# Eight counted ranges in place of seven, 432 counted edge tiles in place of 404, and a larger VectorE budget per slot

## What is computed

```
dst = minimum((12500 * uniform((200000,)) ** 2).astype(int32), ...)   # then sorted
neigh = segment_sum(layernorm(x)[src], dst)            # sum over the edges
h = relu(((1 + eps) * layernorm(x) + neigh) @ W1 + b1) @ W2 + b2
x = x + batchnorm(h)                                   # needs all nodes
x = x + expert_ffn(layernorm(x))                       # routed to one of 8 experts
```

## Time and profile before

| | us |
|---|---|
| median of 3 runs | 2414.71 |
| lowest, highest | 2399.37, 2422.60 |
| the profiled execution | 2417.85 |
| its span, first to last instruction | 2416.2 |
| first gather starts | 118.0 |
| last gather starts | 1594.1 |
| edge stage ends, routing starts | 1629.5 |

### The profile page before, as it was taken

One profiled execution on the slowest core, in us unless ns is written; L12 is line 12 of the kernel. 1 busy time (PEld: TensorE's weight loads), 2 busy tenths in 40 slices (PEclk: granted clock), 3 DMA queues, 4 the chain that ended last, 5 costly groups with the idle time before them and its releaser, 6 DMA issues. The chain is left out here.

```text
span 2416.2 us, 34850 instructions
## 1 busy us (share of the span) xinstructions
PE 1752.9 (73%) x9215; PEld 1075.6 (45%) x9216; DVE 1395.7 (58%) x4228; ACT 917.1 (38%) x1445; POOL 1631.9 (68%) x1606
## 2 busy tenths in 40 slices
PE   0044566767776777778776887688968889799986
PEld 0022233333343333344433443348866556566664
DVE  7886642762753725525435332336865677857886
ACT  5931121431421413324223111116856455365643
POOL 1077777777777777777776777733655677568765
PEclk9998788878888888899898999995759989999998
DMA  6744458458457476584663663517932230321130
GB/s 222 264 136 121 139 166 277 140 164 278 140 183 259 131 246 219 175 267 120 194 212 111 207 197 106 149 47 224 283 126 90 91 93 19 101 90 57 63 100 23
DMA packets 186052, 376.43 MB, mean 156 GB/s; under 512 B 42806, under 2 KB 106636, under 8 KB 185831
## 3 DMA queue, kind: packets, MB, share of 16 engines
q1 hardware_dynamic: 118518, 198.24, 25.1%
q0 software_dynamic: 65168, 174.38, 23.7%
q10 hardware_dynamic: 2144, 1.05, 0.2%
HBM read 306.11 MB, written 71.64 MB: 156 GB/s over the span
## 5 line engine op out<-in xcount | busy, mean ns | idle before, releaser
L907 POOL DMA_INDIRECT space<-table,space x1159 | 1114.2, 961 | 392.4 <-issue 343.8
L1002 PE MATMUL e_sums<-space 128*128 128x256 f16 x1728 | 291.4, 341 | 301.9 <-DVE space L1279 143.6
L1002 PEld LDWEIGHTS e_sums<-space 128*128 128x128 f16 x1728 | 205.1, 121 | 395.4 <-issue 229.6
L1921 POOL TENSOR_TENSOR space<-space 128x512 f16<-128x512 f32 x200 | 293.9, 1495 | 109.0 <-ACT space L2055 103.7
L1268 DVE SCALAR_TENSOR_TENSOR space<-e_sums,above,space 128x256 f32 (+1 forms) x151 | 72.5, 480 | 487.5 <-PE e_sums L1002 329.2
L1163 ACT ACTIVATE counts<-e_tally 128x392 f32 (+1 forms) x296 | 203.9, 689 | 319.3 <-PE e_tally L1042 263.0
L1051 PE MATMUL e_tally<-w1f,counts 128*128 128x512 f16 x686 | 202.0, 424 | 130.7 <-DMA w1f<-table 130.3
L1331 DVE TENSOR_TENSOR counts<-counts,e_tally 128x98 f32 x296 | 175.0, 591 | 150.5 <-ACT counts L1163 105.7
L2011 PE MATMUL x_down<-space 128*128 128x256 f16 x2208 | 251.1, 276 | 14.9 <-DVE space L2148 13.0
L2055 ACT ACTIVATE space<-x_up,b_two 128x512 f32<-128x512 f32 (+1 forms) x400 | 249.0, 691 | 23.7 <-PE x_up L1987 13.9
L1987 PE MATMUL x_up<-space 128*128 128x512 f16 (+1 forms) x1200 | 252.1, 369 | 3.2 <-ACT space L2055 3.2
(11 more groups left out here) (214 smaller groups left out, 2334.9 us busy)
## 6 DMA issues: line engine op xcount, KB each, us to landing
w1f<-table SPq DMA_DIRECT2D x168, 512.0 KB
counts<-in_x SPq DMA_DIRECT2D x48, 512.0 KB, 4.9
space<-table,space POOLq DMA_INDIRECT x1159
slot_rows<-space SPq DMA_DIRECT2D x64, 268.0 KB
space<-slot_rows SPq DMA_DIRECT2D x32, 536.0 KB, 7.0
table<-space SPq DMA_DIRECT2D x25, 512.0 KB, 3.0
out<-space SPq DMA_DIRECT2D x24, 512.0 KB, 3.9
w1f<-in_w SPq DMA_DIRECT2D x8, 1024.0 KB, 5.1
```

What stands on the lines that cost most here:

```text
L907: pool.indirect_dma_start(got[:, r, t, :], None, table.rearrange("p h d -> (p h) d"), bass.IndirectOffsetOnAxis(ap=idx[:, h, first + t:fir ...
L1002: ins = nc.tensor.matmul(sums[:, place, 0:D], hot[:, place, t, :], got[:, r, t, half * D:(half + 1) * D], start=(t == 0 and half == 0), st ...
L1921: nc.gpsimd.tensor_tensor(midl[:, j % 2, c, :], midf[:, c % MB, :], midh[:, j % 2, c, :], ALU.subtract).then_inc(s_mlo, 1)
```

## The change

The counted tiles go from 404 to 432 in eight ranges, the due slots of the quads are earlier by 2 to 4, and the planner's budget for DVE goes from 9.6 to 11.2 us. No instruction is written anew.

```diff
-UNITS = (152, 64, 50, 41, 36, 32, 29)
+UNITS = (152, 64, 50, 41, 36, 32, 30, 27)
...
-CLOSE = {2: 19, 3: 30, 4: 39, 5: 48, 6: 55, 7: 63, 8: 69, 9: 76, 10: 82, 11: 88, 12: 94, 13: 99, 14: 104, 15: 109,
-         16: 114, 17: 118, 18: 123, 19: 127, 20: 132, 21: 136, 22: 140, 23: 144}
-TENSOR_ROOM, VECTOR_ROOM, BEHIND = 1040, 960, 300
+CLOSE = {2: 15, 3: 26, 4: 35, 5: 44, 6: 52, 7: 59, 8: 66, 9: 72, 10: 79, 11: 84, 12: 90, 13: 95, 14: 100, 15: 105,
+         16: 110, 17: 115, 18: 119, 19: 124, 20: 128, 21: 132, 22: 137, 23: 141}
+TENSOR_ROOM, VECTOR_ROOM, BEHIND = 1040, 1120, 300
```

## The result

| | before | changed |
|---|---|---|
| median, us | 2416.81 (4 runs) | 2450.84 (4 runs) |
| lowest, highest | 2399.37, 2422.60 | 2442.16, 2463.23 |
| profiled execution | 2417.85 | 2452.32 |
| first pieces begin | slot 20, 336.4 | slot 16, 297.0 |
| edge stage ends | 1629.5 | 1655.7 |

The ratio is 1.0157, interval [1.0113, 1.0201]: slower by 1.6%. The forecast was 2468, its range 2434 to 2505.

The account below looks back on a forecast made before the run. POOL's gathers looked like the bound, but PE and DVE's equally long chain would set the time: 296 + 1190 + 195 ends the edge stage at 1681, +51.5; 2417.85 + 51.5 = 2469, stated as 2468 us, range 2434 to 2505.

Parts of the forecast that it names:

- Two chains: Edge stage: POOL's gathers, 35 us less if unheld, and PE with DVE, which hold POOL about 100 us and set the time.
- Start of the chain: First 16 slots, 9 to 10 tiles each: POOL still paces them; pieces start in slot 16 at 296 us, not 336.4.
- Pieces: Stretches where table pieces are loaded and multiplied: eight in place of seven, 82 us each, 656 in all.
- second rival: Piece stretches: held POOL frees DMA engines, 77 us each, total 2429, within 1%; sign is stretches under 78; chance 0.13.
- Tiles of ranges 1 to 6: Counted-tile stretches: nearly the same tiles in 39 slots in place of 51, 461 us in place of 505.6.
- The slot: Tile stretches of ranges 1 to 6: each slot less saves its gathered group, 2.8 us (1.92 to 3.59); 12 save 34.
- The quarter: Tile stretches: each quarter less, four PE matmuls beside DVE's tiles, saves 0.6 us (0 to 1.2), 10 us in all.
- Range 7: The added eighth range's tile stretch: 27 wide tiles in 5 slots, 73 us, priced from range 6's 84.5.
- Sum of the chain: Slots 16 to 123: 656 + 461 + 73 = 1190 us for 107 slots, 11.1 each, where POOL needs 1070.
- Rest of the stage: Last 19 slots of the edge stage: 195 us in place of 200.7, so the stage ends at 1681, +51.5.
- Rival 3: Slots with 7 or 8 tiles: one more 3.00 us counting stall each, half showing, 42 us, total 2510; chance 0.12.
- Rival 4: Plan refused on the device, general path runs, if a range spans over 128 targets; 0.02 left out.

Follow-up runs that it names:

- second profile: The changed kernel run again unaltered, beside the kernel before on a chip like the first: 2451.16 us against 2415.99, ratio 1.0149.

## Why the prediction was right, and where it was off

*Two chains, the one behind PE and DVE sets the time.* Right. Had POOL stayed the bound, the last gather would have started near 1594.1 - 35 = 1559, not at 1619.2. The waits for PE were forecast to rise from 9.4 to about 100 us; the same row has 70.4, and with the waits that end at PE's sequencer (L1025; 8.9 before) it is 86.8 in place of 18.3. Of these, 82.3 fall in slots 26 to 122, as forecast.

*Start of the chain.* Forecast 296, measured 297.0 (299.2 in the second profile). The 16 slots have 9 or 10 tiles, the last one 7 (the forecast had 9 to 10 in all); they take 153.0 / 16 = 9.6 us each, as the 20 slots did before (192.4 / 20). Gathers there take 117.05 / 119 = 0.984 us, against 146.68 / 151 = 0.971 in the earlier trace rows: beside the denser one-hots they are 0.01 us longer each.

*Pieces.* Forecast 656, 82 each; measured 654, 81.7 each, and the closeness is in part luck. The sign was 80 to 84 us each, and two of the eight are within it (81.4 and 83.2). Those of ranges 0 to 3 take 314.5 us, 13.5 under the forecast, and are below the 80.2 that I had as the lowest, in the second profile too; the last two are 84.8 and 90.1, together 10.9 over it. One, 77.6, is under the 78 that I had named as the second rival's sign. The seven ranges that both kernels have took 563.9 us in place of 586.8, 22.9 less. That may be the second rival's quieter gather queue, or the slots and quarters that went out of these stretches (ranges 1 and 2 have one slot and two quarters less each); no run parts them. The premise that the loads set most of a stretch didn't hold for their size on the slower chip, where half the bytes left it nearly as long.

*Tiles of ranges 1 to 6: the term that was mis-sized.* Forecast 461, measured 439.2 (89.4, 75.9, 67.3, 59.3, 79.7, 67.6), 22 lower. The term has two prices, 2.8 us for each removed slot and 0.6 for each removed quarter, and the second was too low, in range 1 the first too.

The slot: range 1 comes nearest to measuring it, with the same 64 tiles and the same 8 quarters in 8 slots in place of 11: 101.2 - 89.4 = 11.8, 3.9 us a slot (11.1 and 3.7 in the second profile). A batch-norm pair, 1.3 us of DVE, has moved out of the stretch as well; without it 3.3 to 3.5 are left, near my upper bound of 3.59. I had priced PE's gathered group and, as an alternative to it, DVE's one-hots. DVE's share also holds the two adds of the gathered sum. The one-hots (L1279) and then the adds (L1268) in range 1's tiles, before:

```profile
417.10:518.30 101.20, 16.32 (x88) 0.81 0.44 136
...
417.10:518.30 101.20, 9.54 (x22) 0.81 0.44 136
```

and in the changed kernel:

```profile
376.10:465.50 89.40, 11.41 (x64) 0.81 0.41 128
...
376.10:465.50 89.40, 6.27 (x15) 0.81 0.41 128
```

16.32 - 11.41 = 4.9 and 9.54 - 6.27 = 3.3 over three slots: 2.7 us of DVE a slot. With the pair that moved, DVE is busy for 9.3 us less (79.10 to 69.76), and the idle part of the stretch shrank by the rest. DVE is busy for 78% of the stretch both times, so in this range what a slot takes off DVE comes off the stretch, and somewhat more.

The quarter: I had taken half a group of 16, 1.2 us, as its upper bound. The trace before shows it dearer on PE. The eight quarters of range 2's tiles by their two lines, L1074 and L1084 (PE, PEld busy):

```profile
603.00:690.30 87.30, 7.62 (x16) 2.87 (x16) 0.80 0.43 128
...
603.00:690.30 87.30, 7.67 (x16) 3.14 (x16) 0.80 0.43 128
```

That is 15.3 us, 1.9 each; over all 72 quarters of the six stretches it is 2.0. And in ranges 2 to 6 the stretch shrank by about what PE's busy time shrank. From the earlier trace rows and the stretches above:

| range | stretch shorter by, us | PE's busy time less by | DVE's | slots, quarters less |
|---|---|---|---|---|
| 2 | 11.4 | 11.5 | 5.3 | 2, 4 |
| 3 | 9.5 | 10.1 | 6.4 | 2, 4 |
| 4 | 4.1 | 4.7 | 6.1 | 2, 2 |
| 5 | 12.7 | 12.0 | 3.3 | 1, 2 |
| 6 | 16.9 | 14.1 | 9.9 | 2, 4 |
| sum | 54.6 | 52.4 | 31.0 | 9, 16 |

Of PE's 52.4 us the sixteen quarters are some 33 and the nine gathered groups some 20. Range 5, whose stretch had a clock of 0.98 in place of 0.91, also lost PE time on work that stayed. The second profile has 50.8 us shorter and 48.7 us less of PE. So behind range 1 the price follows PE, and by this reading the quarter, taken at 0.6, is the larger part of the miss. It rests on two profiles; no run changes a quarter or a slot alone. The sum can't decide it either: 3.9 a slot and 1.2 a quarter give 12 x 3.9 + 16 x 1.2 + 2 - 1.6 = 66.4, 2.8 and 2.0 give 66.0, and 505.6 - 439.2 = 66.4 was measured.

*Range 7.* Forecast 73, measured 69.2: the same two prices once more.

*Sum of the chain.* Forecast 1190 for 107 slots, measured 1459.4 - 297.0 = 1162.4, 10.9 a slot. That is +1 at the start, -2 pieces, -22 tiles, -4 range 7: slot 123 starts 27 us before the forecast 1486, and the last gather at 1619.2, 27 before the forecast 1646. The slots of range 1, 8 tiles each, take 89.4 / 8 = 11.2 us in the mean, within the forecast of 11 to 13.

*Rest of the stage.* Forecast 195, measured 196.3. *Behind it*: forecast unchanged, 8 us more, scatter as said. So the stage came 25 us early, the rest 8 late, and the total 17 below the forecast: a part of the miss was covered by 8 us that the forecast had no reason for.

*Rival 3, more stalls in fuller slots*, gave 2510 and didn't come: the fuller slots were cheaper than forecast. *Rival 4*: the plan ran as planned.

*What the experiments add.* On the slower chips packing costs by itself (seven ranges with the new budget, +1.0 and +2.0%), and the eighth range pays where its work is spread (four times -1.0 to -1.4% against the kernel before). For the chip of the result the split above stands on two profiles, and no edit was tried there.

## What to carry to other kernels

Before you move work off the busiest engine, cut the trace where the kind of work changes and add up the length of the stretches: a second chain that is as long will show, with a buffer of a few slots hiding it, and its waits are the first number to rise. Price the removal of a pipeline step with everything each engine does in it, each price read from its own lines in the trace and not by likeness to another instruction, and then look in every stretch which engine's sum the length follows: here it was DVE in one range and, as far as two profiles tell, PE in five. A planner that fits more into a slot moves work and doesn't shorten it: try the same plan spread wider before you judge the work added.

## What was unexpected in the hardware

The same program takes 2416 us on one chip and 2789 to 2813 on two others. Routing and the experts take some 4% longer there (818.9 to 825.3 us in the profiles of the kernels that compute everything, in place of 787 to 795), the changed kernel's edge stage a fifth (1988.5 in place of 1655.7). The gathers themselves take the same time: 949 ns in the median beside 946. On POOL the difference stands in the waits (the changed kernel, slower chip; columns as for the same line above):

```profile
L907 POOL DMA_INDIRECT space<-table,space x1131: 943/949/1764, 118.2 to 1942.2; - x189
its engine sat idle before it (us, times) until:
  issue: 324.1, 1010
  PE e_sums L1002: 228.9, 55
  PEq L1025: 99.7, 27
  remote: 88.4, 37
  DMA space<-rows_of: 29.9, 2
```

"remote" is an end of a wait for which the profile names no work of this core. Such standstills are found on DVE and ACT too, in the first slots already (timeline, start and length, in brackets the idle time before):

```profile
224.19 0.61 ACT L1163 ACTIVATE counts<-e_tally 128x392 f32 x1 [5.87 <-remote]
...
236.53 0.37 DVE L1318 TENSOR_SCALAR w2f<-iota,key 128x490 f16<-128x490 f16 x1 [3.64 <-remote]
```

A slot with up to 10 tiles takes 12.6 us there and 9.6 on the first chip (153.0 / 16). The standstills leave no record of what ran meanwhile. PE is slower too: in these 16 slots its granted clock is 0.68 in place of 0.82, and for the same matmuls it is busy for 119.20 us in place of 97.10. Whether the lower clock is a cause of the standstills or comes of them isn't shown. The cause is open. What follows is only that gains of one kind of chip need not be those of the other: the changed kernel loses 1.5% on the first and nothing that can be measured on the second.
